# Cross attention's strips filled by DMA, and the constants' loads moved under the line attention

## The reference

```
x = x + L0_attn(norm(x))            # 16 heads, scores of line (Pluecker) coordinates, causal
x = x + L0_xattn(norm(x), ctx, ctx) # 16 heads of 16, softmax over 375 keys, with biases
x = x + L0_ffn(norm(x))             # 8 experts, top 2
x = x + L1_attn(norm(x))            # linear attention, 8 heads, rotary, 5-tap convolution, gate
x = x + L1_xattn(norm(x), ctx)      # 16 heads of 16, no biases
x = x + L1_ffn(norm(x))             # 8 experts, top 1
```

## Time and profile before

| | |
|---|---|
| median of 3 runs | 1864.52 us (1863.36 to 1865.52) |
| profiled execution, its time | 1871.49 us |
| profiled execution, its span | 1869.8 us |
| granted TensorE clock, mean | 0.872 |
| PE busy | 1468.9 us, 79% of the span |
| DVE busy | 776.9 us, 42% |
| ACT busy | 585.8 us, 31% |
| POOL busy | 392.8 us, 21% |
| constants loaded, line attention starts | about 69 us |
| line attention ends, cross attention of layer 0 starts | about 246 us |
| cross attention of layer 0 ends | about 617 us |
| cross attention of layer 1 | about 1247 to 1624 us |

### The profile page before, as it was taken

One profiled execution on the slowest core, in us unless ns is written; L12 is line 12 of the kernel. 1 busy time (PEld: TensorE's weight loads), 2 busy tenths in 40 slices (PEclk: granted clock), 3 DMA queues, 4 the chain that ended last, 5 costly groups with the idle time before them and its releaser, 6 DMA issues. The chain is left out here.

```text
span 1869.8 us, 35694 instructions
## 1 busy us (share of the span) xinstructions
PE 1468.9 (79%) x14148; PEld 1154.9 (62%) x14148; DVE 776.9 (42%) x1839; ACT 585.8 (31%) x1278; POOL 392.8 (21%) x456
## 2 busy tenths in 40 slices
PE   0578778999998649999953666648999998759996
PEld 0355536767666539999942555535766766548995
DVE  1355534555552152222243666654455454132223
ACT  0166614455543112222200211213555554112220
POOL 0366510000000124444443111110000000104443
PEclk9699969999998559999976878858999999559997
DMA  7000000000000129999920000000000000109994
GB/s 187 20 1 2 2 1 2 2 2 2 2 2 2 40 89 335 331 325 330 324 91 28 0 0 0 0 0 1 2 2 2 2 2 2 40 6 350 331 325 130
DMA packets 47133, 154.82 MB, mean 83 GB/s; under 512 B 6207, under 2 KB 28063, under 8 KB 32672
## 3 DMA queue, kind: packets, MB, share of 16 engines
q0 software_dynamic: 21120, 130.53, 19.6%
q1 hardware_dynamic: 19868, 19.42, 3.5%
q10 hardware_dynamic: 6020, 3.07, 0.6%
HBM read 140.16 MB, written 12.85 MB: 82 GB/s over the span
## 5 line engine op out<-in xcount | busy, mean ns | idle before, releaser
L849 DVE TENSOR_REDUCE xa_mx<-xa_ps_s 112x2 f32<-112x750 f32 x256 | 240.5, 940 | 259.1 <-PE xa_ps_s L611 258.7
L617 PE MATMUL xa_ps_p<-xa_qs,xa_kT 32*125 32x112 f32 x3072 | 240.9, 288 | 60.0 <-DVE xa_mx L849 48.9
L617 PEld LDWEIGHTS xa_ps_p<-xa_qs,xa_kT 32*125 32x125 f32 x3072 | 197.9, 189 | 140.9 <-issue 69.4
L769 ACT ACTIVATE xa_p<-xa_ps_p 125x672 f32<-125x672 f32 x256 | 187.2, 731 | 225.8 <-PE xa_ps_p L617 225.8
L611 PE MATMUL xa_ps_s<-xa_kT,xa_qT 32*112 32x375 f32 x1024 | 231.5, 528 | 9.4 <-DVE xa_mx L849 9.2
L1443 PEld LDWEIGHTS ex_ps_h<-ex_xT,ex_w 128*128 128x128 f32 x1792 | 212.7, 195 | 10.2 <-DMA ex_w<-in_experts0a,ex_now 3.7
L1443 PE MATMUL ex_ps_h<-ex_xT,ex_w 128*128 128x128 f32 x1792 | 213.3, 278 | 6.6 <-DMA ex_w<-in_experts0a,ex_now 3.3
L1454 PE MATMUL ex_ps_y<-ex_w,ex_hT 128*128 128x256 f32 x896 | 202.7, 379 | 0.0
L1454 PEld LDWEIGHTS ex_ps_y<-ex_w,ex_hT 128*128 128x128 f32 x896 | 165.9, 190 | 20.2
L1477 ACT ACTIVATE ex_hT<-ex_ps_h,ex_w 128x128 f32<-128x128 f32 x224 | 70.2, 364 | 267.8 <-PE ex_ps_h L1443 262.9
L1489 DVE TENSOR_SCALAR ex_hT<-ex_ps_h,ex_w 128x128 f32<-128x128 f32 x224 | 68.3, 347 | 177.8 <-PE ex_ps_h L1443 162.3
(11 more groups left out here) (262 smaller groups left out, 2145.3 us busy)
## 6 DMA issues: line engine op xcount, KB each, us to landing
ys<-ex_y SPq DMA_DIRECT2D x56, 128.0 KB
xn<-rt_xn SPq DMA_DIRECT2D x8, 448.0 KB
load_cin<-in_ctx ACTq DMA_DIRECT2D x4, 750.0 KB
x<-in_x SPq DMA_DIRECT2D x1, 1792.0 KB
out_x<-x SPq DMA_DIRECT2D x16, 112.0 KB
wq_x<-in_wq_x SPq DMA_DIRECT2D x2, 512.0 KB
w_l<-in_w_l SPq DMA_DIRECT2D x1, 1024.0 KB
ex_xg<-xn,ex_now POOLq DMA_INDIRECT x56
```

The costliest lines, as they stand in the source:

```text
L617: return pe.matmul(bp[0:CT, i, c * S:(c + 1) * S], kT[r:r + 32, b % KB, n, c * CT:(c + 1) * CT], qs[r:r + 32, b % 2, n, :], start=True, st ...
L769: act.activation(p[slot % 4][:, :, :], bp[0:CT, :, 0:NC3 * S], ACT.Exp).then_inc(exped, 1)
L849: dve.tensor_reduce(mx[:, b % 2, 2 * pair:2 * pair + 2], bsc[0:S, :, 0:CL], AX, ALU.max).then_inc(maxed, 1)
```

## The change

In cross attention, the weights are no longer padded. Two key matmuls of 128x375 a row (`keys(b, m)`) and eight query instructions fill compact tiles `kU` and `qU`. SP then spreads them to the strips by DMA, to every second partition: four DMAs for the keys, two for the queries, one of zeros for the strip row that will hold the maxima. The other strip rows of `kT` are ones, set once. The negated maxima are turned by one transpose, copied by ACT to `nmT`, and laid by four DMAs into that strip row of `qT` itself. `shifted_queries`, `qs` and the four transposes are gone. `kT` and `qT` have three buffers each. The scale of 1/4 moves into the copy of the queries, which DVE does in both layers. The order between the rounds is new: keys' first half after slot 0, queries after 1, context values after 3 and 4, keys' second half and the turn of the maxima after 5, output turn after 6, turn of x (three rows ahead) and output product after 7. `finish` of a row comes two slots later on DVE.

The context is turned on the host (`ctxT`). `load_constants` is now SP's part of the line attention's block, on four groups of semaphores (x in four parts; 4, 12 and 8 DMAs). Moments and root of x come in groups of four rows at iterations 0 to 2, the first constant row is made after the first projection, the second at the start of cross attention.

In `combine` the bias is added with the first weighted row, the sum is kept beside x, and x is added last; row statistics come one row later.

```diff
 def load_constants(sp, g, A):
+    for n in range(4):
+        rows = slice(4 * n, 4 * n + 4)
+        sp.dma_start(g.x[:, rows, :], A["x"][rows].rearrange("b t d -> t b d")).then_inc(g.x_in[n], 16)
+    sp.dma_start(g.w_l0[:, :, :], ...).then_inc(g.line_in, 16)
+    sp.dma_start(g.wo_l0[:, :, :], ...).then_inc(g.line_in, 16)
+    sp.dma_start(g.bv[:, :], A["bv"]).then_inc(g.line_in, 16)
+    sp.dma_start(g.rows[:, :, :], ...).then_inc(g.line_in, 16)
...
+    for n in range(4):
+        sp.dma_start(g.cT[:, 4 * n:4 * n + 4, :], A["ctxT"][:, 4 * n:4 * n + 4, :]).then_inc(g.cross_in, 16)
 # line attention, PE
             def project(b):
                 pe.wait_ge(x_t, b + 1)
                 reused(pe, v_copied, b)
+                if b == 0:
+                    pe.wait_ge(g.line_in, 16 * LINE_DMAS)
+                if t == 0:
+                    constant_row()
 # line attention, DVE
             for t in range(NB + 5):
+                if t < 3:
+                    row_stats(t + 1)
+                if t == 1:
+                    dve.wait_ge(crow_made, 1)
+                    dve.tensor_copy(g.crow[:, 0, :], b_out[0:S, 0:D]).then_inc(crow_set, 1)
 # cross attention, SP
+            def spread_k(b, m):
+                sp.wait_ge(k_copied, 2 * b + m + 1)
+                reused(sp, shifted, PAIRS * (b - RB + 1))
+                sp.wait_ge(ones_set, b % RB + 1)
+                for k in range(2):
+                    sp.dma_start(kT[0:P:2, b % RB, 2 * m + k, :], kU[64 * k:64 * k + 64, b % 2, m, :]) \
+                        .then_inc(k_spread[RB * m + b % RB], 16)
+            def spread_q(b):
+                sp.wait_ge(q_copied, b + 1)
...
+                sp.dma_start(qT[1:P:32, b % RB, :, :], zeros[:, :, :]).then_inc(q_spread[b % RB], 16)
+                for k in range(2):
+                    sp.dma_start(qT[0:P:2, b % RB, k:QUADS:2, :], qU[64 * k:64 * k + 64, b % 2, :, :]) \
+                        .then_inc(q_spread[b % RB], 16)
+            def spread_nm(b):
+                sp.wait_ge(nm_copied, b + 1)
...
+                for j in range(4):
+                    sp.dma_start(qT[32 * j + 1:32 * j + 2, b % RB, :, :], nmT[QUADS * j:QUADS * j + QUADS, b % 2, :]) \
+                        .then_inc(nm_spread[b % RB], 16)
+            for t in range(-2, NB):
+                if on(t + 2):
+                    spread_k(t + 2, 0)
+                    spread_q(t + 2)
+                if on(t + 1):
+                    spread_nm(t + 1)
+                if on(t + 2):
+                    spread_k(t + 2, 1)
 # cross attention, PE
                     if slot == 0:
-                        pe.wait_ge(qs_made, t + 1)
+                        pe.wait_ge(nm_spread[t % RB], 16 * NM_DMAS * (t // RB + 1))
...
                     if sp == 0:
-                        pe.wait_ge(q_copied, sb + 1)
-                    if sp % 2 == 0:
-                        pe.wait_ge(k_copied, QUADS * sb + sp // 2 + 1)
+                        pe.wait_ge(q_spread[sb % RB], 16 * Q_DMAS * (sb // RB + 1))
+                    if sp % 4 == 0:
+                        pe.wait_ge(k_spread[RB * (sp // 4) + sb % RB], 16 * K_DMAS * (sb // RB + 1))
...
+                round_of(t, 5)
                 if on(t + 2):
+                    keys(t + 2, 1)
                 if on(t + 1):
+                    shift_turn(t + 1)
+                round_of(t, 6)
...
 # combine, DVE
+                dve.scalar_tensor_tensor(yg[:, b, 0, :], yg[:, b, 0, :], g.wtop[:, 0, b:b + 1], bias(b), ...)
+            def add_rest(b):
+                dve.wait_ge((first, second)[top - 1], b + 1)
+                dve.tensor_tensor(g.x[:, b, :], g.x[:, b, :], yg[:, b, top - 1, :], ALU.add).then_inc(x_summed, 1)
```

More of the change, by code:

```diff
@@ L148, in persistent @@
     g.yrow = sb("yrow", [S, 2, NB], I32)
+    g.loads = Phase(nc, "loads")
+    g.x_in = g.loads.sem("x0", "x1", "x2", "x3")
+    g.line_in, g.cross_in, g.rest_in = g.loads.sem("line", "cross", "rest")
     return g
@@ L319, in line_attention, with _ @@
     with nc.Block() as block:
+        @block.sync
+        def _(sp):
+            load_constants(sp, g, A)
         @block.tensor
@@ L386, in u_turn, with constant_row @@
                 last.then_inc(u_turned, 1)
-            pe.wait_ge(set_v, 5)
-            pe.wait_ge(set_p, 2)
+            def constant_row():
+                pe.wait_ge(spread, 1)
+                for c in range(2):
+                    pe.matmul(b_out[0:S, 0:D], g.bvb[:, c, :], g.wo_l0[:, c, :], start=(c == 0), stop=False)
+                pe.matmul(b_out[0:S, 0:D], g.ones[0:1, 0:S], g.rows[0:1, 0, :], start=False, stop=True).then_inc(crow_made, 1)
+            pe.wait_ge(ident_set, 3)
             for t in range(NB + 5):
@@ L665, in queries @@
             def queries(b):
                 pe.wait_ge(x_t, b + 1)
-                for n in range(QUADS):
+                for m in range(2):
                     for c in range(2):
-                        last = pe.matmul(ba[0][:, n * S:(n + 1) * S], g.wq_x[:, layer, c, n * P:(n + 1) * P], xT[:, c, :],
+                        last = pe.matmul(bx[:, m * S:(m + 1) * S], g.wq_x[:, layer, c, m * P:(m + 1) * P], xT[:, c, :],
                                          start=(c == 0), stop=(c == 1))
@@ L719, in out_product @@
                 last.then_inc(out_made, 1)
-            pe.wait_ge(set_v, 2)
-            pe.wait_ge(set_p, 1)
-            for t in range(-2, NB + 1):
+            pe.wait_ge(set_v, 2 - layer)
+            pe.wait_ge(v_set, 1)
+            if layer == 0:
+                pe.wait_ge(g.cross_in, 16 * CROSS_DMAS)
+                for c in range(2):
+                    pe.matmul(bm[0:S, 0:D], g.bvb[:, 2 + c, :], g.wo_x[:, 0, c, :], start=(c == 0), stop=False)
+                pe.matmul(bm[0:S, 0:D], g.ones[0:1, 0:S], g.rows[0:1, 1, :], start=False, stop=True).then_inc(crow_made, 1)
+            for t in range(-3, NB + 1):
                 round_of(t, 0)
```

467 lines of the change are left out of this document (220 added, 247 removed).

## The result

The changed kernel takes 1748.07 us (median of 4 runs, 1747.26 to 1750.24), the kernel before 1865.02 beside it. The ratio is 0.9374, 95% interval 0.9358 to 0.939: 117 us gained. The forecast was 1699, a gain of 166. The direction was right, and so was the mechanism at the start and in the middle of cross attention; at cross attention's two ends it was not, and the cross attentions gave 58 us of the 112 that I counted on.

What follows compares the result with a forecast made beforehand. PE was taken to set the pace in cross attention. Gains of 112 (cross attentions) and 57 (start) less 3 (combine) made 166 off the profiled 1871.5, and 7.0 for the runs' median gave 1699 us; range 1676 to 1745.

Steps and rivals of the forecast that it cites:

- the 112 that I counted on: Both cross attentions together: 56 us gained a layer, 112 us for both, bounds 94 to 125.
- The start: Ahead of the line attention: first projection moves from 75.6 to 14 us; net gain 57 us, bounds 46 to 59.
- A row: Middle of cross attention: a row goes from 20.24 to 16.7 us; total gain 51 us a layer.
- The maxima: Cross attention: the maxima's DMAs land 5.75 us after slot 5's start, before the next slot 0 at 6.2; cost 0.
- Rival 1: Cross attention: maxima land late, PE waits at each slot 0, 30 to 60 us given back, 1745 us; chance 0.2.
- the 0.4 us of cover: Cross attention: margin claimed between the maxima's landing and the next slot 0, 0.4 us.
- The keys' second half: Cross attention: its DMAs land about 6.6 us after slot 5's start, the next slot 1 starts at 8.4; nothing charged.
- The lead-in: Opening of cross attention: a slot with queries falls from 6.3 to about 3.3 us; 5 us gained a layer.
- In the lead-in PE is at the low clock: Opening of cross attention: step that read a 6.3 us slot with queries at low clock and priced it at about 3.3.
- The tail: End of cross attention: iteration 14 loses only its long slot 6, a gain of 1.4 us a layer.
- Combine: Combine, with the constant row: costs 3 us in all, bounds minus 8 to plus 9.

Runs made afterwards that it cites:

- `maxima_last`: Changed kernel with SP issuing the two DMAs of the keys' second half before the four of the maxima: 1777.68 us, ratio 0.9508.
- `changed_again`: The changed kernel, unaltered, run again on another chip: 1741.72 us, ratio 0.9352.
- `lead_fill`: Changed kernel plus PE matmuls nobody reads in cross attention's lead-in, behind the first queries and each round with scores alone: 1724.69 us, ratio 0.9216.
- `old_work`: Changed kernel plus, for rows 0 and 1 only, as many unread matmul columns on PE as the change took away: 1722.24 us, ratio 0.9257.
- `all_six`: Changed kernel plus unread matmuls in lead-in and tail, maxima's turn before keys' second half, earlier second constant row, memsets off first row's path: 1694.81 us, ratio 0.9059.

## Why the prediction was right and wrong

**The start: right.** First projection at 12.18 us, 14 forecast; first `exterior` at 18.18, 6.0 behind it, 6.9 forecast. The line attention ends at 187.2, 59.5 earlier; 57 forecast, 46 to 59 the bounds. `cross_back`, which has the start without the new cross attention, ends it at 187.1.

**A row: right within 0.15 us.** Forecast 16.7, measured 16.86, and 16.83 without late landings. Slots 1, 3, 5 and 6 are 2.03 to 2.04, slot 2 2.12 (2.11 forecast), slot 7 2.07. Slot 0 is 2.37 for 2.27, slot 4 2.17 for 2.04. Over 26 rows 0.13 us more is 3 us.

**The maxima: right in the result, wrong in the margin.** An issue took 0.57 to 0.63 us, not 0.37, so the four take 2.55 and not 1.5; PE goes on 1.7 us after the last issue begins. PE's weight load waits 0.4 us a row for them, but slot 7 is 2.07 where a bare slot is 2.03, so that costs 0.04. Rival 1 as written, waits at each slot 0, did not happen; `maxima_last` shows that 1.1 us more would have brought it nearly in full, so of the 0.4 us of cover nothing was left, and that the kernel did not pay for it was close to luck.

**The keys' second half: wrong.** I gave 8.4 - 6.6 = 1.8 us of slack and charged nothing. A usual landing (2.2) left 0.5 of it: the landings of 3.3 to 4.0 us lengthen slot 0 by 0.65 to 1.35. The four issues ahead had taken 1 us more than I gave them, and a landing varies from 2.0 to 4.3 us. Iterations 1 to 13 are 4.2 and 7.0 us longer than the 218.8 without such waits: 11 us, in a place where I had named no rival. How many landings are late is chance (9 here, 14 in `changed_again`, 3 in `lead_fill`).

**The lead-in: wrong, and the largest part.** Forecast 5 us less a layer, measured 11.5 and 11.4 more (7.6 + 3.9 and 7.4 + 4.0, the first part and iteration -1): 33 us in all. The failed step is "In the lead-in PE is at the low clock", read from one stretch and priced there alone, with nothing set down for the other rounds. The slot that I priced came out right: slot 1 of iteration -1 takes 3.5 us, 3.3 forecast, 5.6 before. But before, the clock was at 1.00 for half of the lead-in, as the stretches between 246 and 293 us would have shown, and the six slots behind that one took 1.93 to 2.03; after, at 0.50, they take 2.64 to 3.53. `lead_fill` takes back 11.3 and 10.7 us, 22 of the 33. Why the changed kernel is left at 0.50 is open: that it lacks the removed matmuls is the obvious guess, and `old_work` did not bear it out. Nor do low clock and idle PE go together in the rows, as the prediction has it: before, PE is busy for all of 270 to 273 at 0.53, and for 1.83 of the 3 us from 258 to 261 at 1.00. The other part is a term put at nothing: the memsets at the stage's opening, which were in the diff and which I did not price. The first norm ends 9.0 us behind the stage's start, before it was 3.7; taken out of the way (`all_six`) they give 5.7 us a layer, 11 of the 33, 5.3 of the 5.7 in the norm of layer 1.

**The tail: wrong.** Forecast -1.4 a layer, measured +3.2 and +1.8: 8 us. The clock again: it falls 12 us after the start of iteration 14, and in `changed_again` 20 us after it, where the tail takes 42.9 and 43.4 and the forecast's sign is right. So the size of this term is luck.

**Combine: wrong in sign by the profiles, nothing by the runs.** The 7.7 us of the stage table are pauses of the profiled execution. The stages other than combine sum to 116.2, the medians differ by 117.0. I forecast +3; it is between -1 and +1.2, the latter the difference of the orders where both were seen with pauses (some 53.0 and 51.8).

The sum of what was missing: 33 (lead-in) + 11 (late landings) + 3 (slots) - 1 (iteration 0, which gained 4.0 and 4.4 where I gave a row 3.5) + 8 (tail) - 2.5 (start) - 3 (combine) + 1 (other stages) = 49.5, against 49 between 1699 and 1748.

## What to carry to other kernels

When a change takes work from the engine that sets the pace, read the granted clock of the stretches at both ends of the stage as well as in its middle: here rounds that had run at 1.00 ran at 0.50 behind the change, whatever took the clock away, and fewer matmuls took longer. Some 16 matmuls that nobody reads gave 11 us a layer back. A list of memsets at a stage's opening has a price if the first instruction on the path is DVE's. And a slack against a DMA is to be compared with its longest landing, not its usual one.

## What the runs showed of the hardware

- Transfers within SBUF to every second partition, 94 KB: 0.57 us to issue and 2.2 to land; the rows of before for stores had 0.33 and 1.6. One of 1.8 KB costs the same issue, 0.60. The Trainium skill ("DMA: Bandwidth & Descriptors", "Anatomy of one DMA — SWDGE (gpsimd) path") gives a fixed 2.0 us for a DMA issued from GpSimd; the 2.2 measured here for SP's, which have 94 KB to move besides, are near it.
- A single packet of the instruction queue (16 KB) that begins while such a transfer is under way comes with a landing 1.0 to 2.1 us later. This is read from 52 iterations of two traces (23 late ones, 19 of them with the packet at 1.73 to 2.02 us); it was not provoked.
- A DVE instruction of 0.41 us took 5.73 beside five memsets of POOL, and 0.41 again once they stood behind it.
- DVE paused in multiples of 0.70 us beside POOL's gathers in combine of layer 0, on two of three chips, 8 us in all.
- The clock fell 12 us after the start of iteration 14 in one execution of the changed kernel and 20 after it in another, with tails 7.0 and 5.0 us apart. The two kernels with all the fillers and the new order spread over 2 and 4 us; the changed one over 3 in its first four runs and over 12 in the next five.
